# Scores, maxima and small products of the attention phases written as products of 32 output rows

## What is computed

```python
q = heads(norm(x) @ Wq + bq); k, v = heads(ctx @ Wk + bk), heads(ctx @ Wv + bv)
attn = softmax(einsum('bhnd,bhsd->bhns', q, k) * 8 ** -0.5)
x = x + gate * (einsum('bhns,bhsd->bhnd', attn, v) @ Wp + bp)
```

## Time and profile before

| what | value |
|---|---|
| median of 3 runs | 6477.11 us |
| profiled execution, its own time | 6475.3 us |
| its span, first to last instruction | 6473.5 us |
| PE, weight loads (PEld), DVE, ACT, POOL busy | 92%, 48%, 64%, 65%, 15% |
| matmul records of PE, and weight loads | 49,714 and 49,714 |
| granted TensorE clock over the span | 0.98 of full speed (2.4 GHz) |
| HBM traffic | 62 GB/s over the span |

### The profile page before, as it was taken

The page is one execution under the profiler, slowest core; times in us unless marked ns, Lnnn a source line. Parts: engine busy times, 40 slices in busy tenths (PEclk is TensorE's granted clock), DMA queues, the critical chain, the costliest instruction groups (busy, mean ns, idle before and its releaser), DMA issues.

```text
span 6473.5 us, 147216 instructions
## 1 busy us (share of the span) xinstructions
PE 5939.3 (92%) x49714; PEld 3112.4 (48%) x49714; DVE 4119.5 (64%) x6523; ACT 4237.2 (65%) x8158; POOL 981.5 (15%) x1660
## 2 busy tenths in 40 slices
PE   6999999999877899999999977789999999999998
PEld 3444444444444444544454444444444444445665
DVE  5767677677555667766776445467777777754443
ACT  3777777777666577777777556557777777773333
POOL 3121121121111111111111011212212212200000
PEclk9999999999999899999999989899999999999999
DMA  2322322222111322232232011122232232220110
GB/s 88 78 65 56 79 59 63 75 56 69 42 57 61 82 68 65 69 79 69 57 76 75 1 57 57 55 77 68 57 77 68 57 77 68 57 65 21 54 53 29
DMA packets 180915, 402.05 MB, mean 62 GB/s; under 512 B 16992, under 2 KB 124560, under 8 KB 166416
## 3 DMA queue, kind: packets, MB, share of 16 engines
q1 hardware_dynamic: 180752, 400.01, 22.9%
HBM read 316.81 MB, written 83.14 MB: 62 GB/s over the span
## 4 chain that ended last, share of the span: by engine, by line
PE 73%; issue 8%; ACT 8%; DVE 7%; DMA 2%; SPq 1%; POOL 1%; ACTq 0%; DVEq 0%; POOLq 0%
PE bank L1140 19%; PE bank L1186 18%; PE pair L1156 14%; DVE MX L1480 3%; PE bank L1112 2%; ACT P L1316 2%; PE bank L1107 2%; DMA QP<-scr_q 2%; PE pair L1173 2%; PE pair L1162 1%; PE bank L699 1%; PE bank L690 1%; ACT QP L1327 1%; PE pair L626 1%; DVE ST L1437 1%
## 5 line engine op out<-in xcount | busy, mean ns | idle before, releaser
L1316 ACT ACTIVATE P<-bank 128x512 f32<-128x512 f32 (+1 forms) x5504 | 3102.2, 597 | 1350.6 <-PE bank L1140 1306.9
L1480 DVE TENSOR_REDUCE MX<-pair 128x2 f32<-128x802 f32 x3072 | 2923.9, 988 | 1296.3 <-PE pair L1156 1288.0
L1140 PE MATMUL bank<-QP,KP 128*128 128x256 bf16 (+1 forms) x11008 | 2091.3, 277 | 141.7 <-ACT P L1316 90.0
L1186 PE MATMUL bank<-P,VA 128*25 128x256 f32 (+1 forms) x22016 | 1756.0, 391 | 5.8 <-issue 0.5
L1156 PE MATMUL pair<-KP,QP 96*128 96x401 bf16 x6144 | 1576.0, 338 | 60.9 <-DMA QP<-scr_q 42.3
L1140 PEld LDWEIGHTS bank<-QP,KP 128*128 128x128 bf16 (+1 forms) x11008 | 858.0, 100 | 1577.3 <-ACT P L1316 912.9
L1186 PEld LDWEIGHTS bank<-P,VA 128*25 128x25 f32 (+1 forms) x22016 | 401.7, 102 | 711.0 <-issue 456.7
L1156 PEld LDWEIGHTS pair<-KP,QP 96*128 96x128 bf16 x6144 | 593.5, 98 | 181.7 <-DVE MX L1480 64.0
L1605 POOL COPY VA<-VN 128x416 f32<-128x416 f32 (+1 forms) x320 | 138.6, 434 | 2520.6 <-PE bank L1186 2439.1
L1484 DVE TENSOR_REDUCE MX<-pair 128x4 f32<-128x1024 f32 x256 | 311.3, 1223 | 326.8 <-PE pair L1162 326.2
L1327 ACT CAST QP<-pair 2x512 bf16<-2x512 f32 x640 | 338.9, 575 | 130.1 <-PE pair L1173 124.7
(11 more groups left out here) (246 smaller groups left out, 4497.5 us busy)
## 6 DMA issues: line engine op xcount, KB each, us to landing
KP<-scr_k SPq DMA_DIRECT2D x192, 900.6 KB
QP<-scr_q SPq DMA_DIRECT2D x960, 48.0 KB
CN<-ctx_n SPq DMA_DIRECT2D x40, 768.0 KB
scr_k<-KSF SPq DMA_DIRECT2D x48, 600.8 KB, 3.3
scr_k<-KSF SPq DMA_DIRECT2D x48, 600.0 KB, 3.3
CT<-ctx_t SPq DMA_DIRECT2D x24, 800.5 KB, 4.4
KP<-scr_ks SPq DMA_DIRECT2D x128, 144.0 KB
scr_q<-QS SPq DMA_DIRECT2D x80, 192.0 KB, 2.1
```

Source lines behind the costliest of these rows:

```text
L1140: last = nc.tensor.matmul(SC[half][0:kt, k * N:(k + 1) * N], KP[g][:, c0:c0 + kt], QP[g][:, h * N:(h + 1) * N], start=True, stop=True)
L1186: last = nc.tensor.matmul(OB[32 * h:32 * h + STEP + HD + 1, 0:N], VA[g % 2][0:kt, t, h, :], P[(g * ph.nt + t) % 2][0:kt, h * N:(h + 1) * N ...
L1316: nc.scalar.activation(P[v % 2][0:kt, half * 2 * N:(half + 1) * 2 * N], SC[half][0:kt, :], ACT.Exp, scale=SCALE).then_inc(sem("probs_full" ...
L1480: nc.vector.tensor_reduce(MX[:, r, c:c + 2], MP[j % 2][:, :].rearrange("p (t k) -> p t k", t=2)[:, :, 0:SPANS[0][1]], AX.X, ALU.max).then_ ...
```

## The change

PE alone is changed. A new function, `strips_of`, writes one product as up to four, each with 32 columns of the stationary operand and so with 32 output rows; `start` and `stop` are the same for each strip. Scores, maxima, and the pieces var, q, keys, values, d, e and y call it. The mean, the transposes, the value products and the shift rows stay as they are.

```diff
+            def strips_of(out, lhsT, rhs, start=True, stop=True):
+
+                n = lhsT.shape[1]
+                for c in range(0, n, 32):
+                    m = min(32, n - c)
+                    last = nc.tensor.matmul(out[c:c + m, :], lhsT[:, c:c + m], rhs, start=start, stop=stop)
+                return last
+
...
                 elif name == "var":
                     pe.wait_ge(sem("squared"), at("squared", b, 1))
-                    last = nc.tensor.matmul(MISC[:, 0:N], w("mean"), SQ[:, 0:N], start=True, stop=True)
+                    last = strips_of(MISC[:, 0:N], w("mean"), SQ[:, 0:N])
...
                     for k, t in enumerate(range(4 * int(name[1]), min(4 * int(name[1]) + 4, ph.nt))):
                         kt = ph.tiles[t]
-                        last = nc.tensor.matmul(MISC[0:kt, k * D:(k + 1) * D], src[:, t * 128:t * 128 + kt],
-                                                w(ph.name + "wv"), start=True, stop=True)
+                        last = strips_of(MISC[0:kt, k * D:(k + 1) * D], src[:, t * 128:t * 128 + kt], w(ph.name + "wv"))
...
                     c0 = h * ph.nk + t * 128
-                    last = nc.tensor.matmul(SC[half][0:kt, k * N:(k + 1) * N], KP[g][:, c0:c0 + kt],
-                                            QP[g][:, h * N:(h + 1) * N], start=True, stop=True)
+                    last = strips_of(SC[half][0:kt, k * N:(k + 1) * N], KP[g][:, c0:c0 + kt],
+                                     QP[g][:, h * N:(h + 1) * N])
...
                         h, qt, (c0, n) = j // 4, j // 2 % 2, SPANS[j % 2 * 2 + k]
-                        last = nc.tensor.matmul(MP[j % 2][:, k * 512:k * 512 + n],
-                                                QP[g][0:MR, h * N + qt * 128:h * N + qt * 128 + 128],
-                                                KP[g][0:MR, h * ph.nk + c0:h * ph.nk + c0 + n], start=True, stop=True)
+                        last = strips_of(MP[j % 2][:, k * 512:k * 512 + n],
+                                         QP[g][0:MR, h * N + qt * 128:h * N + qt * 128 + 128],
+                                         KP[g][0:MR, h * ph.nk + c0:h * ph.nk + c0 + n])
```

More of the change, by code:

```diff
@@ L1094, in piece @@
                     pe.wait_ge(sem(done), at(done, b, 1))
-                    last = nc.tensor.matmul(MISC[:, 0:N], w(ph.name + "wq"), XM[:, 0:N], start=True, stop=True)
+                    last = strips_of(MISC[:, 0:N], w(ph.name + "wq"), XM[:, 0:N])
                     if not ph.cross:
-                        last = nc.tensor.matmul(MISC[:, N:2 * N], w(ph.name + "wk"), XM[:, 0:N], start=True, stop=True)
+                        last = strips_of(MISC[:, N:2 * N], w(ph.name + "wk"), XM[:, 0:N])
                 elif name[0] == "t":
@@ L1106, in piece @@
                         pe.wait_ge(sem("ctx_loaded"), at("ctx_loaded", b, 16))
-                    last = nc.tensor.matmul(MISC[:, 0:n], w(ph.name + "wk"), CT[:, c0:c0 + n], start=True, stop=True)
+                    last = strips_of(MISC[:, 0:n], w(ph.name + "wk"), CT[:, c0:c0 + n])
                 elif name[0] == "v":
@@ L1116, in piece @@
                     for c in range(2 * NPAIR):
-                        last = nc.tensor.matmul(MISC[:, c * 2 * G:(c + 1) * 2 * G], RS[:, c * 128:(c + 1) * 128], w("pick"),
-                                                start=True, stop=True)
+                        last = strips_of(MISC[:, c * 2 * G:(c + 1) * 2 * G], RS[:, c * 128:(c + 1) * 128], w("pick"))
                 elif name == "e":
@@ L1121, in piece @@
                     for c in range(2 * NPAIR):
-                        last = nc.tensor.matmul(MISC[:, c * 128:(c + 1) * 128],
-                                                RDX[:, c * 128:(c + 1) * 128], w("ident"), start=True, stop=True)
+                        last = strips_of(MISC[:, c * 128:(c + 1) * 128], RDX[:, c * 128:(c + 1) * 128], w("ident"))
                 elif name == "y":
                     for p in range(NPAIR):
-                        last = nc.tensor.matmul(MISC[:, 0:N], w(ph.name + "wp", p * D, D), ON[:, p * N:(p + 1) * N],
-                                                start=(p == 0), stop=(p == NPAIR - 1))
+                        last = strips_of(MISC[:, 0:N], w(ph.name + "wp", p * D, D), ON[:, p * N:(p + 1) * N],
+                                         start=(p == 0), stop=(p == NPAIR - 1))
                 last.then_inc(sem("misc_full"), 1)
@@ L1161, in maximum @@
                         for qt in range(2):
-                            last = nc.tensor.matmul(MP[j % 2][:, (2 * k + qt) * N:(2 * k + qt + 1) * N],
-                                                    QP[g][0:MR, h * N + qt * 128:h * N + qt * 128 + 128],
-                                                    KP[g][0:MR, h * ph.nk:(h + 1) * ph.nk], start=True, stop=True)
+                            last = strips_of(MP[j % 2][:, (2 * k + qt) * N:(2 * k + qt + 1) * N],
+                                             QP[g][0:MR, h * N + qt * 128:h * N + qt * 128 + 128],
+                                             KP[g][0:MR, h * ph.nk:(h + 1) * ph.nk])
                 last.then_inc(sem("max_full"), 1)
```

## The result

The changed kernel takes 6710.16 us (median of 4 runs, 6690.46 to 6720.57) where the kernel before takes 6477.19 us on the same chip: a ratio of 1.0357, 95% interval 1.0332 to 1.0382. The prediction was 6399 us: it had the sign wrong, and the result lies 50 us above its range. The profiled execution has a span of 6704.8 us.

The account below looks back on a forecast made before the run. PE was taken to set the pace of the cross elements. Savings of about 523 us less costs of about 437 gave 86 us; less a tenth, 6477 - 78 = 6399 us, range 6290 to 6660.

Parts of the forecast that it names:

- step 1: Value products in a cross element: the stops at changes between 128-row and 32-row products go, 52 x 0.19 = 9.9 us saved.
- step 2: Scores and maxima of a cross element: each wave of four strips costs 0.017 us more than one product, +5.7 us.
- the strips go freely: Rival, all strips: each starts once its quarter of the array is free, a wave costs its stream alone; 6050 us, 10%.
- step 3: Small products of a cross element: 58 passes pay 0.017 us each, +1.0 us; d's narrower weight loads save 0.5 us.
- step 4: Mean and transposes of a cross element stay at 128 rows between strips: new changes of mode, +1.0 us.
- step 5: PE's loop body grows to some 16 code blocks, perhaps fetched every element: 0.08 us a block, at most +1.3 us.
- The prediction's own sign of being wrong: At a code block boundary, PE idle over 0.2 us with "issue" as cause would show the forecast wrong.
- rival "Code": Rival, PE's loops: code blocks come too late and cost 0.5 us each, 336 us instead of 55; 6680 us, 13%.
- The sum: All 80 attention elements: savings of about 523 us less costs of about 437 leave 86 us.
- a tenth given back: Of the 86 us saved, a tenth is lost where a faster PE only waits longer for ACT's exponentials.
- the 25 ns of its Part 1: Least distance between two matmul starts; every wave would cost 55 ns more, 1.2 ms in all; 2% of the slow-wave rival's 14.

Follow-up runs that it names:

- x1: The kernel before, without strips, with PE's loop over the middle elements written as two elements a pass: 6539.57 us, ratio 1.0105.
- x6: The kernel before with strips for scores and maxima only in five slots (29, 31, 33, 44, 46) of each cross element: 6475.11 us, ratio 1.0001.
- x5: The kernel before with strips for scores and maxima only in three slots (29, 31, 33) of each cross element: 6460.06 us, ratio 0.9973.
- x10: The changed kernel without most of the bulk loads of keys and context in the cross elements (output not the reference's): 6329.38 us, ratio 0.9761 of the kernel before.
- x7: The kernel before with strips for scores and maxima only in slots 26 to 51 of each cross element: 6676.89 us, ratio 1.0308.

## Why the prediction was wrong, step by step

**Removed stops (step 1): right.** 0.09 is gone before the values, and values to score is down by 0.13, of which some 0.02 belongs to the next step.

**Waves (step 2): wrong, in the kernel's favour.** "The second wave waits for the last of the first" took the 0.23 between two groups of four for a property of waves. In the new slot eight strips take as long as two whole products, and the value block is down to 0.43, two waves of 0.215; the 0.02 went with the change of mode ahead of the block. The term of +5.7 is about 0. This is the mechanism of the rival "the strips go freely", which got 10%.

**Small products (step 3)**: nothing in the traces speaks against it, and no run isolates them. **New changes of mode (step 4): right.** In the loops of the changed kernel the mean, which stays whole between strips, starts 0.264 us after the start of the last strip before it, and the next score 0.309 after the start of the mean's last pass; the same distances were 0.172 and 0.215. The transposes, where nothing else is waited for, have 0.266 and 0.202 for 0.173 and 0.109. So there is a stop of 0.09 on each side of both, and it is the plainest sign that the stop comes from the change of mode.

**Code (step 5): the step that failed.** "At most +1.3 in an element by these rows, which I take" priced a block at 0.08 us. The loop's first pass, from which that came, fetches at the pace of whole products and over 7 blocks, and says nothing of strips beside 80% busy DMA engines. Measured in the changed kernel: 278 us of stops and some 123 us of half clock in 42 elements, 9.5 us an element, 0.56 us for each of its 17 blocks. The prediction's own sign of being wrong, a block boundary with over 0.2 us of idle PE and "issue" as its cause, came over a hundred times. The rival "Code" (13%) had a price of 0.5 us a block and 6680 us. The price was close, the mechanism only half: it named the fetch, not the loads it collides with, nor the clock that falls after the stop, and it kept the +5.7 of step 2, so that the nearness of 6680 to the 6710 measured is in part luck. In x1 it was 0.2 us a block, nearly all of it at the jump; in x6 357 more blocks than in x5 ate the 15 us by which x5 is faster than x6, and what slots 44 and 46 bring.

**The sum.** Without stops and half clock the loops would take 4274.5 - 401 = 3874 us, 180 under the kernel before or 4.3 us an element (an estimate from these counts), against the 2.7 to 3.5 that the prediction had without code. But the gain is smaller than the slots promise. In elements of x10, set against the earlier trace rows:

```profile
885.60:982.10 96.50, 84.65 (x2017) 53.00 (x2005) 70.02 (x112) 72.54 (x137) 19.01 (x32) 1.00 0.09 27
2912.80:3000.90 88.10, 82.17 (x2015) 52.45 (x2011) 65.69 (x82) 69.35 (x132) 13.42 (x19) 1.00 0.12 39
```

PE's work in an a0 element falls by 9.6 us, from 94.22 to 84.65, and the element by 2.1. PE stands 11.9 us instead of 4.4: 2.2 of it are stops for code, 3.6 waits for exponentials (1.7 before) and 2.3 waits for the reductions of the maxima (0.4 before). In c1, which has no context to prepare, the element keeps 5.4 us. So "a tenth given back" was far too low in a0: there the other engines' chains, not their busy shares, took over.

## What to carry to other kernels

An instruction costs more than its time on the engine. Count the body of a loop before instructions are multiplied: here PE kept a body of 2035 of them and fetched one of 2077 anew in each pass. When it no longer fits, put dense runs of short instructions where the DMA engines are quiet, and check the timeline for an engine that stops in the middle of a product with "issue" as its cause, with the DMA share in that window and the granted clock behind it. And a saving need not be applied everywhere: 15 of 52 slots gave 1.6%, all of them lost 3.6%.

## What was not expected of the hardware

A late block of code stops PE for up to 5.2 us in the changed kernel (5.6 in x7), where the packet takes some 1.2. After the stop of slot 36 the granted clock was 0.50 for some 5 us of full work (1023.8 to about 1029). In all, the loops of the changed kernel have 283 us at 0.50, in 59 stretches, and those of the kernel before none. A change between 128-row and 32-row products cost 0.09 to 0.10 us wherever it was measured. Four strips of 32 rows run at the pace of one product of 128, with starts 2 to 5 ns apart (907.750, .752, .757, .759). The Trainium skill (TensorE: Matmul & The Clock Gate, Part 3, Measured speedup vs the span model) has about 4 ns of issue from one tile of the array to the next. The trace agrees; the 25 ns of its Part 1, which the prediction weighed in a rival, don't apply to strips in different quarters.
